# ScalarE's order of exponentials and moves in the attentions that have one PSUM bank of turned probabilities

## The reference, cut to what matters

```python
scores = jnp.einsum('bhqd,bhkd->bhqk', q, k) / np.sqrt(HEAD_DIM)
scores = jnp.where(causal, scores, -jnp.inf)
attn = jax.nn.softmax(scores, axis=-1)
out = jnp.einsum('bhqk,bhkd->bhqd', attn, v)
```

## Time and profile before

| | us |
|---|---|
| median of 3 runs | 2785.68 (2785.33 to 2793.83) |
| the profiled execution's own time | 2778.91 |
| its span | 2777.1 |
| PE busy in the span | 2281.8 (82%) |
| DVE, ACT, POOL busy | 1396.8, 975.9, 362.1 |
| stretch with the 16 attentions of layer 0 | about 140 to 1200 |

### The profile page before, as it was taken

The page is one execution under the profiler, slowest core; times in us unless marked ns, Lnnn a source line. Parts: engine busy times, 40 slices in busy tenths (PEclk is TensorE's granted clock), DMA queues, the critical chain, the costliest instruction groups (busy, mean ns, idle before and its releaser), DMA issues. The chain is left out here.

```text
span 2777.1 us, 39594 instructions
## 1 busy us (share of the span) xinstructions
PE 2281.8 (82%) x13818; PEld 1620.3 (58%) x13875; DVE 1396.8 (50%) x4005; ACT 975.9 (35%) x3080; POOL 362.1 (13%) x638
## 2 busy tenths in 40 slices
PE   8678888888898888968136788898989888898988
PEld 4356566565777655757014566665656666665755
DVE  6245546465444553221295555554656555554651
ACT  3123434444353433422002343233334333233331
POOL 1043242351414150000000000000000000000000
PEclk9667878898989988989567899999999999999997
DMA  7000000002223013446500000000000000000000
GB/s 282 8 4 1 5 8 5 8 9 77 77 82 111 24 32 113 154 158 227 155 20 10 8 2 8 6 8 5 5 8 2 8 6 9 5 8 5 1 4 4
DMA packets 50765, 116.30 MB, mean 42 GB/s; under 512 B 8192, under 2 KB 30464, under 8 KB 46976
## 3 DMA queue, kind: packets, MB, share of 16 engines
q1 hardware_dynamic: 49024, 109.49, 11.8%
q0 software_dynamic: 1536, 4.20, 0.5%
HBM read 90.20 MB, written 23.46 MB: 41 GB/s over the span
## 5 line engine op out<-in xcount | busy, mean ns | idle before, releaser
L689 ACT ACTIVATE PRS<-PT 128x384 f32<-128x384 f32 (+1 forms) x512 | 264.3, 521 | 476.6 <-PE PT L620 476.4
L752 DVE TENSOR_REDUCE negmax<-SM 128x2 f32<-128x512 f32 x432 | 283.8, 686 | 232.2 <-PE SM L583 168.8
L704 ACT ACTIVATE PRS<-SM,negmax 128x128 f32<-128x128 f32 x608 | 249.3, 421 | 261.5 <-DVE negmax L752 261.5
L620 PE MATMUL PT<-const_sb,PRS 128*128 128x128 f32 x1664 | 281.4, 299 | 25.6 <-ACT PRS L689 18.5
L620 PEld LDWEIGHTS PT<-const_sb,PRS 128*128 128x128 f32 x1664 | 208.2, 153 | 84.4 <-issue 55.4
L376 PE MATMUL PJ<-big,arena 128*128 128x256 f32 x832 | 216.6, 408 | 8.5 <-ACT big L2720 8.5
L2556 DVE TENSOR_SCALAR arena<-arena 128x256 bf16<-128x256 bf16 x1024 | 206.0, 282 | 0.6 <-PE SC L2451 0.6
L573 PE MATMUL SM<-KF,QM 32*128 32x256 f32 (+1 forms) x1024 | 138.1, 388 | 69.6 <-ACT PRS L702 47.6
L376 PEld LDWEIGHTS PJ<-big,arena 128*128 128x128 f32 x832 | 165.9, 205 | 44.5 <-ACT big L2720 12.0
L635 PE MATMUL OA<-PRS,VS 128*32 128x256 f32 (+1 forms) x1536 | 189.7, 372 | 0.6 <-ACT PRS L689 0.6
L573 PE MATMUL SM<-haloU,QM 32*128 32x128 f32 (+1 forms) x1056 | 172.9, 373 | 13.2 <-ACT PRS L704 10.7
(11 more groups left out here) (521 smaller groups left out, 3972.8 us busy)
## 6 DMA issues: line engine op xcount, KB each, us to landing
arena<-lay SPq DMA_DIRECT2D x50, 1024.0 KB, 4.9
arena<-lay SPq DMA_DIRECT2D x1, 7700.5 KB, 32.6
rows<-OT SPq DMA_DIRECT2D x2, 3456.0 KB, 32.3
arena<-lay SPq DMA_DIRECT2D x1, 3862.0 KB, 19.6
arena<-rows SPq DMA_DIRECT2D x25, 128.0 KB, 2.5
arena<-lay SPq DMA_DIRECT2D x25, 128.0 KB, 5.0
rows<-arena SPq DMA_DIRECT2D x25, 128.0 KB, 4.4
rows<-OT SPq DMA_DIRECT2D x1, 2432.0 KB, 21.9
```

Source lines behind the costliest of these rows:

```text
L620: ins = pe.transpose(bank[:, o:o + P], PR[n % 4][:, t, k * P:(k + 1) * P], ident)
L689: act.activation(dst, src, ACT.Copy).then_inc(S("probs_moved"), 1)
L704: ins = act.activation(dst, src, ACT.Exp, bias=negmax[:, h, r:r + 1], accum_out=rsum[:, t, h:h + 1])
L752: st.post(dve.tensor_reduce(negmax[:, ORDER[s], :], two(banks[s % NB]), AX.X, ALU.max, negate=True), S("max_ready"))
```

## The change

In the two modes with one bank, ScalarE's slot changes from "move, move, exponentials, exponentials" to "exponentials of head 2i, move of head 2i-2, exponentials of head 2i+1, move of head 2i-1". The other engines' programs stay as they are, and so does ScalarE's in layer 1, where `early` was false.

```diff
             for i in range(attention_slots(mode)):
-                early = len(hs.flips) == 1 and mode != "conv"
                 for d in range(2):
                     s = 2 * i + d - ahead
-                    if 0 <= s < H and not early:
+                    if 0 <= s < H:
                         exponentials(s)
                     if lag <= i < PAIRS + lag:
                         move_probs(2 * (i - lag) + d)
-                for s in (2 * i, 2 * i + 1):
-                    if early and s < H:
-                        exponentials(s)
```

## The result

| | before | changed |
|---|---|---|
| median, us | 2785.51 (2756.17 to 2793.83, 4 runs) | 2889.90 (2887.96 to 2893.66, 4 runs) |
| profiled execution, us | 2778.91 | 2887.97 |
| its span, us | 2777.1 | 2886.2 |
| granted clock over the span | 0.875 | 0.865 |

The ratio is 1.040, 95% interval 1.032 to 1.047: the change costs 104 us by the medians and 109 us between the two profiled executions. The forecast was 2908 in a range of 2830 to 2970.

What follows compares the result with a forecast made beforehand. TensorE was taken as the bound in layer 0's attentions. New waits 171.7 less old 56.1 and 5.8 gave +109.8; minus 8 backlog, plus 20 clock, +122 us: 2908 us, range 2830 to 2970.

Steps and rivals of the forecast that it cites:

- (a): At the head of the next scores, TensorE's wait for exponentials goes in every slot with moves: 56.1 of 64.9 us.
- (c): Behind slot 7, the next slot's first transposes no longer wait 6.3 us for exponentials; 5.8 us saved after a part returns.
- (b): Second transposes wait for a move now behind maximum and exponentials, starting 1.39 us after the maximum: 171.7 us of new waits.
- the six classes: 112 slots sorted by near or causal, on time, VectorE late or half clock; new waits 40.3, 28.9, 55.9, 37.6, 7.3, 1.7 us.
- (d): In four or five causal slots 7, the new pause lets VectorE work off its backlog: 8 us off.
- (e): In layer 0's attention stretch, new pauses lower the mean granted clock from 0.85 to 0.83: +20 us.
- Absorption: Rival: pauses take VectorE's lateness out of 24 late slots, which pay 30 us instead of 93.5; 2832 us, chance 0.12.
- The exchange: Rival: in each slot the new wait merely replaces the old one, time within 0.3%; chance 0.03.
- the faster case: Rival: at the second transposes new waits don't show and the old ones go, 62 us less, 2723 us; chance 0.05.
- The clock as the largest part: Rival: the clock falls to 0.74 in all of the attention stretch, +90 us, 2978 us; chance 0.14.
- The signs in the profile: Attention stretch: scores' waits under 15 us, transposes' over 150, clock 0.81 to 0.84, layer 1 unchanged to a few us.

Runs made afterwards that it cites:

- e5: Against the kernel before: ScalarE does both heads' exponentials ahead of both moves; 3111 us, ratio 1.118.
- e2: The changed ScalarE order in layer 0's eight near attentions only, the causal ones as in the kernel before; 2866 us, ratio 1.031 to before.
- e3: The changed ScalarE order in layer 0's eight causal attentions only, the near ones as in the kernel before; 2840 us, ratio 1.021 to before.
- e1: Against the kernel before: ScalarE's slot is move, exponentials, move, exponentials, with the move first; 2715 us, ratio 0.976.
- e6: Kernel before, old order, with VectorE taking the row maximum of each pair's first head twice in layer 0; 2835 us, ratio 1.017.
- e7: Changed kernel with VectorE taking the row maximum of each pair's first head twice in layer 0; 3082 us, ratio 1.105 to before.

## Why the prediction was right, and where it was off

**(a) and (c), the old waits go.** Right. The scores' waits fell by 54.7 us (64.9 to 10.2; 56.1 were forecast), and the first transposes' wait for exponentials (6.3) is gone.

**(b), the new wait.** Right, in place, price and sum. The wait for the move rose by 170 us (18.4 to 188.4) against 171.7 by the six classes. The rule "1.39 us after the maximum" was 1.47 in the late slot shown: from the start of the move to the transposes it took 0.63 us, where I had 0.56. The waits matched all the same (3.96 for 3.95), because the wait is counted from the end of the product with the values, and in the slot of the earlier trace rows the second transposes start 0.06 us ahead of that end. Two small errors cancel there. By kind: the second transposes' waits rose by 109 us in the near attentions (103.5 in the classes) and by 61 in the causal ones (68.2).

**(d), the backlog.** Right in place, and the 8 us did not show in the sum. In the timeline of the changed kernel the second transposes of slot 7 have no wait in the causal attentions of batches 0 to 3, where the classes counted 1.6 to 2.3 us each, 7.9 together (at half clock, so slow matmuls hide a part too); the causal sum is smaller by that. The near attentions' larger waits made up for 5 us of it, so that the wait for the move came out at 170 and not at 171.7 - 8. What took 8 us off the idle time was something I had not counted: waits of the side work itself. In the kernel before, side work waited for VectorE's norm twice, and in the changed kernel this wait isn't in the list:

```profile
PE PJ L1208 <- DVE OUT L428: 8.1, 2, 4.2
```

That the idle time grew by 99.6 us for a forecast of 101.8 is in part luck.

**(e), the clock.** Right in size, by luck in part, and by a model that is too simple. I took +20 us from a fall of 0.02; TensorE's busy time rose by 21.4 us with a fall of 0.03, for which my price gives 28. My price of 9.4 us for 0.01 gives 66 us for the fall from 0.82 to 0.75 in e5, and its busy time rose by 114. The mean clock of a stretch is the wrong measure, because it also counts the time in which TensorE stands idle at half clock. The clock records of the traces are at 1.0 or 0.50 at any time. For the kernels with TensorE's program unchanged, in the stretch of the attentions:

| kernel | time at half clock, us | TensorE busy in it | more than before | half of that | busy time in all, more than before |
|---|---|---|---|---|---|
| before | 314.0 | 290.2 | | | |
| changed | 409.6 | 338.4 | 48.2 | 24.1 | 21.4 |
| e2, near half | 409.6 | 355.6 | 65.4 | 32.7 | 33.8 |
| e3, causal half | 389.1 | 353.3 | 63.1 | 31.6 | 32.4 |
| e1 | 257.0 | 234.8 | -55.4 | -27.7 | -23.7 |
| e6 | 416.4 | 379.1 | 88.9 | 44.5 | 46.1 |
| e5 | 704.0 | 569.8 | 279.6 | 139.8 | 135.0 |
| e7 | 710.5 | 587.7 | 297.5 | 148.8 | 142.3 |

The last two columns agree within 7 us: this fits work that takes twice its time at half clock. The changed kernel has the same 409.6 us at half clock as the near half alone, but it is idle for 71 us of them (54 in the near half, 24 before), so less work was slowed. That is why two halves cost 34 and 32 us of busy time and the whole change 21.

The clock of single attentions went both ways. The near attentions of batches 2 and 5 before,

```profile
345.00:412.00 67.00, 61.21 (x383) 44.70 (x385) 32.01 (x70) 23.21 (x86) 29.82 (x58) 0.73 0.01 5
...
693.00:766.00 73.00, 65.37 (x502) 51.35 (x503) 36.29 (x85) 29.93 (x114) 30.53 (x59) 0.95 0.23 77
```

and in the changed kernel:

```profile
352.00:421.00 69.00, 51.44 (x391) 38.30 (x389) 33.55 (x74) 22.64 (x86) 29.73 (x58) 0.88 0.01 5
739.00:827.00 88.00, 74.04 (x509) 57.71 (x512) 36.46 (x86) 29.75 (x115) 30.45 (x59) 0.86 0.20 65
```

The first rose from 0.73 to 0.88 and cost 2 us more in all, with its new waits; the second fell from 0.95 to 0.86 and cost 15 us more. The forecast of 20 us was right as a sum over many such places, and says nothing of one of them.

**The distance to 2908.** The forecast difference was +122, the one of the profiled executions +109, by the medians +104. The stretch itself came out at 99.6 + 21.4 = +121 us, for 101.8 + 20. The missing 12 us lie behind it, 8.3 between the last attention and layer 1 and 3.3 in layer 1. Nothing of the change is there; the kernels with other edits show 303 or 308 to 312 us for the first of these pieces. What makes it one or the other was not tried.

**The rivals.** Absorption would have had waits of the transposes near 127 us (18.4 + 171.7 - 63.5); they are 188, and a delay of the maximum goes straight to the path (e6 against e7). The exchange and the faster case fall with that. The clock as the largest part is wrong for this change, 21 of 121 us. On the way from the changed kernel to e5 and e7 it is the larger part (114 us of busy time and 98 of idle time; 121 and 66), and so it is from the kernel before to e6 (46 and 13).

**The signs in the profile.** They came: the scores' waits are under 15 us, those of the transposes over 150, the clock of the stretch is 0.82, layer 1 is 3.3 us shorter, and an on-time near slot without side work at full clock took 5.62 us (5.53 before; 5.5 to 5.7 was forecast).

## What to carry to other kernels

When an in-order engine serves two chains, ask of each order which instruction now stands behind the slowest input, and what the waiting engine has queued behind it; a wait that was covered by independent work isn't exchanged for one of equal length ahead of that work, it is added to it. Put the job whose input is there already (the move) first, while the other input (the maximum) is still being made: that order was worth 2.4% here and the opposite one cost 4%. And measure idle and busy time of the bound engine apart: here the idle time of two edits added up, and the busy time went by how much work fell at half clock, which did not add.

## What the runs showed of the hardware

A pause of TensorE can be paid a second time, by work at half clock behind it. Going from the changed kernel to the one with the slower maximum, 66 us more idleness came with 121 us more busy time for the same instructions, at a granted clock of 0.74 instead of 0.82; and 31 us of meaningless matmuls ahead of the scores of 14 slots took 54.5 us off the others, at 0.94 instead of 0.87. The sum of the idle time doesn't give this price: 100 us more of it came with 21 us of busy time in the changed kernel, and 13 us with 46 in e6. "TensorE: Matmul & The Clock Gate" of the Trainium skill says in "A second HAM failure mode: psum-queue depth-cycling" that frequent short pauses between groups of matmuls lower the throughput by the changes of the clock. The runs with the slower maximum and with both exponentials first (0.74 and 0.75) agree with it; in the changed kernel it was true only of a small part, 21 us.

Hand-overs between the engines, from the slots shown: the end of VectorE's maximum to the start of the exponentials 0.03 us, the exponentials' start to the next instruction of ScalarE 0.81, the start of a 128x384 move out of PSUM to the transposes that wait for it 0.63.

The kernel before also scatters by its clock: its runs on one chip went from 2764.8 to 2795.1 us (17 runs), while those of e1 went from 2712.7 to 2719.8 (6 runs).
